# A fixed stretch of rows for every expert, row sends spread over sixteen groups, and VectorE's scans ahead of its low parts

## The reference

```python
# attention: H, DH = 16, 64; latents of 64; rotary positions on all 64 channels of a head
h = layernorm(layernorm(x)) * ln_scale + ln_bias
c_q, c_kv = h @ w_down_q.T, h @ w_down_kv.T
q, k, v = heads(c_q @ w_up_q.T), heads(c_kv @ w_up_k.T), heads(c_kv @ w_up_v.T)
attn = softmax(rope(q) @ rope(k).T / 8)
x = x + layernorm(merge(attn @ v) @ w_out.T + residual)
# experts: E, F = 8, 256, each token takes 2 of 8
z = layernorm(x)
probs = softmax(z @ router)
weights, chosen = top_k(probs, 2); weights = softmax(weights)
y = sum_e full_weights[e] * ((silu(z @ gate[e]) * (z @ up[e])) @ down[e])
x = x + layernorm(y)
```

## Time and profile before

| | us |
|---|---|
| median of 3 runs (1506.58 to 1506.79) | 1506.65 |
| the profiled execution's own time | 1505.08 |
| its span in the trace | 1502.7 |
| PE busy (93%) | 1399.5 |
| POOL busy (81%) | 1216.6 |
| DVE busy (78%) | 1166.6 |
| ACT busy (71%) | 1066.0 |

### The profile page before, as it was taken

One profiled execution on the slowest core, in us unless ns is written; L12 is line 12 of the kernel. 1 busy time (PEld: TensorE's weight loads), 2 busy tenths in 40 slices (PEclk: granted clock), 3 DMA queues, 4 the chain that ended last, 5 costly groups with the idle time before them and its releaser, 6 DMA issues. The chain is left out here.

```text
span 1502.7 us, 45158 instructions
## 1 busy us (share of the span) xinstructions
PE 1399.5 (93%) x17865; PEld 930.2 (62%) x17865; DVE 1166.6 (78%) x2685; ACT 1066.0 (71%) x2072; POOL 1216.6 (81%) x731
## 2 busy tenths in 40 slices
PE   4899999999999999999999999999999988969995
PEld 1366665666666656666665656666666555659995
DVE  7788787777788788877788788777887888945576
ACT  2677787778877877778787777777887765724444
POOL 5588898888888988889889888899789878826275
PEclk8799999999999999999999999999999999979997
DMA  5444443423233324333333323233232242133222
GB/s 169 117 114 114 114 110 84 115 69 82 65 87 83 76 72 107 79 79 79 84 86 87 79 73 88 76 82 83 72 93 67 63 160 67 44 117 99 69 53 81
DMA packets 101489, 132.87 MB, mean 88 GB/s; under 512 B 16673, under 2 KB 51233, under 8 KB 100897
## 3 DMA queue, kind: packets, MB, share of 16 engines
q1 hardware_dynamic: 98208, 123.70, 30.8%
q0 software_dynamic: 3072, 6.30, 1.4%
HBM read 20.49 MB, written 14.94 MB: 24 GB/s over the span
## 5 line engine op out<-in xcount | busy, mean ns | idle before, releaser
L1222 ACT ACTIVATE probs<-psum 128x512 f32<-128x512 f32 x1024 | 615.2, 604 | 190.3 <-PE psum L932 189.1
L1970 POOL TENSOR_TENSOR probs_lo<-probs 128x1024 f16<-128x1024 f32 x301 | 624.8, 2086 | 117.0 <-ACT probs L1222 116.0
L1518 DVE CUSTOM_DVE_ANT_0 scan_out<-psum,ahead 128x512 f16<-128x512 f32 x512 | 349.4, 686 | 199.0 <-PE psum L827 189.7
L951 PE MATMUL psum<-cv,probs 128*128 128x66 f16 x4096 | 476.3, 193 | 12.6 <-POOL probs_lo L1970 12.1
L953 PE MATMUL psum<-cv,probs 128*128 128x64 f16 x4096 | 475.9, 193 | 0.0
L955 PE MATMUL psum<-cv,probs_lo 128*128 128x66 f16 x4096 | 474.6, 192 | 0.0
L953 PEld LDWEIGHTS psum<-cv,probs 128*128 128x128 bf16 x4096 | 380.5, 97 | 110.7 <-issue 3.0
L951 PEld LDWEIGHTS psum<-cv,probs 128*128 128x128 bf16 x4096 | 385.4, 97 | 73.6 <-POOL probs_lo L1970 13.3
L930 PE MATMUL psum<-q_both,k_twice 128*128 128x512 f16 x1024 | 388.8, 380 | 2.8 <-ACT probs L1222 2.8
L932 PE MATMUL psum<-q_max,k_ones 65*128 65x512 f16 x1024 | 391.1, 382 | 0.0
L955 PEld LDWEIGHTS psum<-cv,probs_lo 128*128 128x128 f16 x4096 | 380.0, 98 | 0.0
(11 more groups left out here) (222 smaller groups left out, 1854.8 us busy)
## 6 DMA issues: line engine op xcount, KB each, us to landing
t_swapped<-t_sin SPq DMA_DIRECT2D x248, 128.0 KB, 2.0
k_twice<-qk_hi SPq DMA_DIRECT2D x128, 128.0 KB
q_lone<-qk_hi SPq DMA_DIRECT2D x64, 128.0 KB, 2.3
q_both<-qk_hi SPq DMA_DIRECT2D x64, 128.0 KB
q_both<-qk_lo SPq DMA_DIRECT2D x64, 128.0 KB
q_max<-qk_hi SPq DMA_DIRECT2D x64, 128.0 KB, 2.3
k_ones<-qk_lo SPq DMA_DIRECT2D x64, 128.0 KB, 2.4
z_unit<-slots_in SPq DMA_DIRECT2D x31, 128.0 KB, 2.3
```

What stands on the lines that cost most here:

```text
L951: pe.matmul(acc, high[:, q * P:(q + 1) * P, 1], v[:, 0:VLO], start=opens, stop=False, skip_group_check=True)
L1222: act.activation(probs[s % 4][:, i, :], score_ps[tile % SCORE_BANKS], ACT.Exp, scale=SCALE).then_inc(probs_done, 1)
L1518: dve.tensor_tensor_reduce(scan_out[m % 2][:], bank[BANK_OF["base", n, m]], ahead[m % 2][:], 1.0, LOWEST, ALU.add, ALU.max, max_all[a][:, ...
L1970: pool.tensor_tensor(probs_lo[s % 4][:].rearrange("p a n -> p (a n)"), p, p.bitcast(BF16).rearrange("p (n two) -> p n two", two=2)[:, :, 1 ...
```

## The change

The rows sent and the results now live in one HBM tensor `slots` of 26368 rows: each expert owns 3072 (`MOST_UNITS * UNIT`, as many as three batches could give it), and 1792 stand behind for the units that are not used. An expert's first row is known beforehand, so PE adds it to the ranks with one more product (`base_rows`), and `take_ranks` writes `slot_of` by itself. `place` keeps only what tells where each unit lies (`row_of`) and whose it is (`column_of`). It moves from g29 step 1 to g31 step 10 (`PLACE_AT` (7, 10)), and the ranks from group 4 step 15 of an epoch to group 5 step 10.

The sends go out two a group in g14 to g29, in steps 5 and 15 (one, in step 15, in g19 and g27), and nine each in g30 and g31. Every one but the first of a step 0 also waits for the exponentials of the steps before. From g14 to g29 DVE makes the low part of step 14 as well, a seventh; in g30 it makes eight instead of fourteen, in g31 twelve instead of sixteen, and POOL the others. In DVE's `attend`, `take_maxima` and `scan` now stand ahead of `lagged`, in every group.

SP loads and stores a unit at a row that it reads from `row_of` (one register load for four units, once for loads, once for stores). Clearing takes 26 DMAs of up to 512 KB instead of 8, four a group. The gathers wait two by two for the dense units 2, 3, ... 25.

```diff
@@ sizes, steps and places @@
+SLOTS = E * MOST_UNITS * UNIT
+ALL_SLOTS = SLOTS + (SORTED - CHOICES * MOST_UNITS) * UNIT
...
-LATE_DVE_STEPS = {GROUPS - 3: (2, 4, 6, 8, 10, 13, 15), GROUPS - 2: (0, 1, 2, 3, 5, 6, 7, 8, 9, 11, 12, 13, 14, 15),
-                  GROUPS - 1: tuple(range(STEPS))}
+SENDING = tuple(range(14, 30))
+LATE_DVE_STEPS = {**{g: DVE_STEPS + (14,) for g in SENDING}, GROUPS - 2: (1, 3, 5, 7, 9, 11, 13, 15), GROUPS - 1: (0, 1, 2, 4, 5, 6, 8, 9, 10, 12, 13, 14)}
...
-RANK_AT, PLACE_AT = (4, 15), (5, 1)
+RANK_AT, PLACE_AT = (5, 10), (7, 10)
...
-SEND_AT = ([(LAST - 2, s) for s in (11, 12, 13, 14, 15, 15)]
-           + [(LAST - 1, s) for s in range(STEPS) for _ in range(2 if s % 3 == 0 and s else 1)]
-           + [(LAST, s) for s in range(14) for _ in range(1 + s % 2)])
+SEND_AT = [(g, s) for g in SENDING for s in ((15,) if g in (19, 27) else (5, 15))]
+SEND_AT += [(g, s) for g in (30, 31) for s in (0, *range(1, STEPS, 2))]
+FIRST_GATHER = 2
@@ SP @@
             def load_unit(unit):
+                first = first_row(unit, rows_from)
...
             def store_unit(unit):
+                first = first_row(unit, rows_to)
...
-                    for piece in to_clear[2 * (r - 1):2 * r]:
-                        clear_slots(*piece)
+                    clear_slots(r, 0)
...
+                clear_slots(g, 1)
                 put_both(g + 1, 1)
@@ PE, rank_tokens @@
+                pe.matmul(dst[:, 0:own], ones[:], base_rows[:], start=True, stop=False, skip_group_check=True)
@@ DVE, take_ranks and place @@
-                dve.tensor_reduce(ranks[:, n], rank_parts[:], AX, ALU.add).then_inc(ranked, 1)
+                    dve.tensor_reduce(slot_of[:, n], rank_parts[:], AX, ALU.add).then_inc(ranked, 1)
...
+                dve.tensor_scalar(unused[:], units_of[0:1, :], -float(UNIT), float(MOST_UNITS * UNIT), ALU.mult, ALU.add)
...
+                dve.tensor_tensor(jumps[:], past[:], unused[:].unsqueeze(1).to_broadcast([1, COLUMNS, E]), ALU.mult)
...
+                step(dve.tensor_tensor(row_of[:], jump[:], steps_of[0:1, :], ALU.add), 7)
@@ DVE, attend @@
                 for s in range(STEPS):
-                    lagged(g, s, g > 0)
                     if g and s == TURN_STEPS[1]:
                         take_maxima(g, 1)
...
                         scan(g + 1, s)
+                    lagged(g, s, g > 0)
@@ POOL, sends and gathers @@
                     if (t, k) == (0, 0):
-                        pool.wait_ge(placed, 1)
+                        pool.wait_ge(ranked, n + 1)
                         pool.wait_ge(z_lo_done, CHUNKS * (n + 1))
+                    if 2 * s + i:
+                        pool.wait_ge(probs_done, g * KEY_TILES + 2 * s + i)
...
+                beside = FIRST_GATHER + made // 2
+                if made % 2 == 0:
+                    pool.wait_ge(fuse_done, SORTED + beside + 1)
+                else:
+                    pool.wait_ge(added, beside - DOWN_LAG + 1)
                 fetch(j, t, k)
```

More of the change, by code:

```diff
@@ L492, in final_place @@
             return final_bank(j)[:, at * P:(at + 1) * P]
-        to_clear = [(at, min(clear_rows, SORTED * UNIT - at)) for at in range(0, SORTED * UNIT, clear_rows)]
+        to_clear = [(at, min(clear_rows, ALL_SLOTS - at)) for at in range(0, ALL_SLOTS, clear_rows)]
         cleared, clear_set = sem("cleared"), sem("clear_set")
@@ L566, in in_dram, with unit_rows @@
             return t[bass.ds(b, 1)].rearrange("b (t p) d -> p (b t) d", p=P)
-        def unit_rows(rows, unit):
-            return rows[unit * UNIT:(unit + 1) * UNIT, :].rearrange("(i p) d -> p i d", p=P)
+        def unit_rows(first):
+            return slots[bass.ds(first, UNIT), :].rearrange("(i p) d -> p i d", p=P)
         def dense(unit):
@@ L883, in rank_tokens @@
                 own = TILES * E
+                pe.matmul(dst[:, 0:own], ones[:], base_rows[:], start=True, stop=False, skip_group_check=True)
                 for k in range(CHOICES):
-                    pe.matmul(dst[:, 0:own], above[:], hots[:, n, k].rearrange("p t e -> p (t e)"), start=k == 0, stop=False,
+                    pe.matmul(dst[:, 0:own], above[:], hots[:, n, k].rearrange("p t e -> p (t e)"), start=False, stop=False,
                               skip_group_check=True)
@@ L1668, in take_ranks, with step @@
             def take_ranks(n):
+                def step(ins, k):
+                    ins.then_inc(rank_steps, 1)
+                    dve.wait_ge(rank_steps, n + k)
                 dve.wait_ge(rank_ready, n + 1)
@@ L1674, in take_ranks @@
                     last = dve.tensor_tensor(rank_parts[:, k], before, hots[:, n, k], ALU.mult)
-                dve.tensor_copy(counts[:], src[:, TILES * E:TILES * E + E]).then_inc(rank_steps, 1)
-                dve.wait_ge(rank_steps, n + 1)
+                step(dve.tensor_copy(counts[:], src[:, TILES * E:TILES * E + E]), 1)
                 standing()
-                dve.tensor_reduce(ranks[:, n], rank_parts[:], AX, ALU.add).then_inc(ranked, 1)
+                with nc.allow_low_precision(reason="one of eight parts is not zero, and it is a whole number"):
+                    dve.tensor_reduce(slot_of[:, n], rank_parts[:], AX, ALU.add).then_inc(ranked, 1)
             place_steps = sem("place_steps")
             def place():
-                rows = EARLY * CHOICES * TILES
                 def step(ins, k):
@@ L1707, in place @@
-                step(dve.tensor_tensor(to, base_sum[:, 0:rows], ranks[:, 0:EARLY].rearrange("p b k t -> p (b k t)"),
-                                       ALU.add), 9)
+                step(dve.tensor_tensor(past[:], unit_at[:].unsqueeze(2).to_broadcast([1, COLUMNS, E]),
+                                       unit_ends[0:1, :].unsqueeze(1).to_broadcast([1, COLUMNS, E]), ALU.is_ge), 4)
+                dve.tensor_tensor(jumps[:], past[:], unused[:].unsqueeze(1).to_broadcast([1, COLUMNS, E]), ALU.mult)
@@ L1709, in place @@
+                step(dve.tensor_reduce(expert_of[:], past[:], AX, ALU.add), 5)
+                step(dve.tensor_reduce(jump[:], jumps[:], AX, ALU.add), 6)
+                dve.tensor_scalar(column_of[:], expert_of[:], float(E - 1), float(F), ALU.min, ALU.mult)
+                step(dve.tensor_tensor(row_of[:], jump[:], steps_of[0:1, :], ALU.add), 7)
                 standing()
```

66 lines of the change are left out of this document (34 added, 32 removed).

## The result

The changed kernel is slower: median 1586.12 us (4 runs, 1579.55 to 1590.2) against 1506.62 for the kernel before, a ratio of 1.053 (95% interval 1.051 to 1.055). The forecast was 1469.0, with a range of 1457 to 1485. The profiled execution took 1585.43 us with a span of 1582.3.

A forecast was written before the change was run, and what follows sets the result against it. PE was taken as the bound, apart from stalls in g29 and g30 and the hole before the sorted units; -12.2 - 7.7 - 9.5 - 11 + 3 + 0.5 - 1.5 + 0.8 = -37.6 us gave 1469.0 us, range 1457 to 1485.

The forecast's parts named there:

- The hole: Between g31 and the sorted units: PE starts 5.5 us after the group's end, not 17.66; -12.2 us.
- The clock: Start of the sorted units: shorter PE idling loses less time to the 1.2 GHz level; -1.5 us.
- g29 and g30: Both groups lose their stalls, falling to 38.0 and 36.3 us; -7.7 and -9.5 us.
- Scans ahead of low parts: g0 to g28: PE waits less for scans, turned maxima and rank sums; 60% of 18.2 us, -11 us.
- end of +5: Slow end of the scans' term in g0 to g28: +5 us if low parts come late instead.
- rival 1: Reordering only moves PE's wait to DVE's low parts or divisions; the 11 us are gone, 1480 us; chance 20%.
- keep their 1.21 to 1.26: DVE's low parts beside POOL's sends stay this short (us), so sends pay; the port rule alone would add 3 to 6 us.
- Sends and the seventh low part: g14 to g28: two sends a group, one POOL low part given to DVE, mostly covered by idle time; +3 us.
- g31: DVE makes 13 low parts instead of 16 there but also `place`, counted at 3.9 to 5 us; +0.5 us.
- The small things: SP's register loads, gathers' waits and 18 more clearing DMAs cost nearly nothing; +0.8 us for all.

The follow-up runs named there:

- e9: e8 with `place` moved in one piece to g30 step 1 and DVE making all sixteen low parts of g31; ratio 0.998 to the kernel before.
- e12: e11 with `place` cut into four parts in g30 and DVE making all sixteen low parts of g31; 1486.4 us, ratio 0.987 to the kernel before.
- e8: The changed kernel with DVE's old order (low parts ahead of scans), on a chip of usual speed; 1506.7 us, ratio 1.001 to the kernel before.
- e1: The kernel before with only DVE's reordering (scans and turned maxima ahead of low parts), on a slow chip; ratio 1.039, 61 us slower.
- e6: The kernel before with POOL's low parts only writing zeros, plus DVE's reordering; 1482.9 us, ratio 0.985 (without the reordering 1475.9 us).
- e11: e8 with one wait a group in g14 to g29: POOL's low part of step 3 waits for DVE's of step 2; 1495.2 us, ratio 0.993.
- e7: The changed kernel with POOL's low part of an odd step waiting for DVE's of the step before; 1528.1 us, ratio 1.016 to the kernel before.
- e2: The changed kernel with DVE's old order (low parts ahead of scans), on a slow chip; ratio 0.980 to the kernel before there, 27.5 us faster.

## Why the prediction was wrong, step by step

- **The hole: right in kind, and its sum partly by luck.** PE's first sorted product starts 3.5 us behind the end of g31 (1404.05); I said 5.5, and the last send within a us of the end. The send started 2.6 us ahead of it, and its landing took 3.13 us where I had 2.25. The hole shrank by 14.1 us (12.2 predicted, 13.9 at the most). SP's register load and the arithmetic take 0.8 us, from the landing of the send (1404.59) to the issue of the load (1405.35), as predicted. The chain and PE's first unit (start us, us, what):

```profile
1401.46 3.13 DMA slots<-z_rows,slot_of
...
1404.61 0.51 SPq L673
...
1407.59 0.38 PE L1046 MATMUL psum<-ident_half,z_unit 128*128 128x128 f16 x4 [0.61 <-DMA z_unit<-slots]
```

- **The clock: not as predicted.** I gave it -1.5 us in the sorted units, but they take 92.5 us (before 92.3). Their first stretch did run at a higher clock than in the earlier trace rows:

```profile
1407.59:1413.00 5.41, 4.23 (x26) 3.25 (x27) 1.61 (x4) 0.68 (x2) 0.00 (x0) 0.72 0.57 166
```

Why the whole is no shorter stays open. In e9 and e12, where the clock is 1.00 throughout, the sorted units take 91.2 us. That the part behind g31 shrank by 13.9 us in all, with 13.7 predicted, is two errors that cancel.

- **g29 and g30: right.** Without the reordering (e8) 39.2 and 35.9 us (38.0 and 36.3 predicted), with no wait of 3 us.
- **Scans ahead of low parts: the step that failed.** Predicted -11 us with an end of +5; it is +74.5 (spans of the changed kernel and e8, on two chips; e1 has +61 against its own chip's kernel before). I worked out that a low part "of 1.3 to 2.1" would be in time two steps later. These were durations of the old order, in which DVE's low part seldom began inside one of POOL's (21 of 211). Behind the scan it mostly begins when POOL's own low part is already running, and the 116 held by one take 2.2 to 2.8 us for the most part. The direction stood there as rival 1, but its price, the 11 us gone, supposed unchanged durations as well. So did the end of +5.
- **What was in the rows.** The earlier trace rows has DVE's low parts at 1207/1260/3350, one of 3.15 us. I used the long one as a cause of waits and never asked why the same instruction takes 1.22 us in one place and 3.15 in another. The sentence that low parts "keep their 1.21 to 1.26" beside sends misread that row, too: three of them that began during a send in g30 took 2.6 to 3.4 us. I did weigh the Trainium skill's rule on the shared port ("SBUF — State Buffer", section "SBUF: two separate sides"), but only for sends beside low parts. It says that a VectorE instruction with two SBUF inputs and a GpSimd one that reads SBUF exclude each other for a whole instruction, whichever begins first; my sentence had left out that the GpSimd one must read SBUF. Read for two low parts, it fits the ends of the 180, and the memsets of e6, which read nothing, agree. It goes by one instruction, and the holds of up to four in a row (6.2 us) show more. "Whichever begins first" fails beside a send, as the last section shows.
- **Sends and the seventh low part: +3 predicted, +23.4 measured (e8).** The +3 rested on POOL's idle time, 3.9 us a group. That time was not used up: POOL's waits for ACT there are 60.0 us in e8, 58.8 before (I had expected 38). 13.4 us of the 23.4 are the three holds that one wait a group takes away (e11), so what counts is where POOL pauses and not how much it idles in total. The other 10 are spread over the groups, and no wait of PE in them (e11) is longer than 1.5 us; I did not take them apart.
- **g31: +0.5 predicted, +9.4 measured (e8).** I counted `place` at 3.9 to 5 us and next to nothing for the low parts that stand behind it; with its own pieces held it took 6.3, and PE stood still for 7 us.
- **The small things: right.** g0 to g13 with 18 clears more, +1.5 us in e8; gathers every 1.25 us and 82.2 us from the first of them on.
- In sum, without the reordering I expected -26.6 us and got +5.0 of span; 29 of the 31.6 between them are the sends and g31. With it, 117 us separate forecast and result, three quarters of them (74.5 + 11) from one line moved.

## What to carry to other kernels

When an instruction's shortest and longest time differ by more than a factor of two, find what decides before moving it: here the order on one queue cost little by itself (7 us in e6), and nearly all of the rest came from when its instructions begin beside those of the other queue. If VectorE and GpSimd both read SBUF, count where each one's instructions begin beside the other's. A wait that lets the short one go first can pay (56 us in e7, 12 with one a group in e11). Work moved to a busy group is best moved in pieces (6.9 us between e9 and e12 in g30). A ratio measured on one chip may hold something of that chip: e2 had 0.980 there and 1.001 elsewhere.

## What the runs showed of the hardware that I had not expected

- DVE's low part (two SBUF inputs) is held by a running POOL instruction that reads SBUF, and ends 1.08 us behind it: all 180 over 1.3 us in the changed kernel, all 101 before. Sometimes it is held past two to four POOL instructions in a row (6.2 us at worst). What decides whether DVE gets its turn at the first end of such an instruction (174 of the 180) is open.
- The other way round, a DVE low part that begins while POOL is idle is not held: in the fourteen traces, 375 begin so and have a POOL instruction that reads SBUF begin before they end, and none of them takes over 1.3 us.
- Small instructions are held as well: `unused`, 1x8, 1.71 instead of 0.16 us; `unit_ends`, 128x8, 1.96 instead of 0.15.
- DVE instructions that read PSUM are not held. All scans and all products with the sine, in the changed kernel:

```profile
L1541 DVE CUSTOM_DVE_ANT_0 scan_out<-psum,ahead x512: 637/690/694, 38.5 to 1366.2; 128x512 f16<-128x512 f32 x171
L1529 DVE TENSOR_TENSOR t_sin<-psum,sin_sb x124: 673/680/682, 22.0 to 1307.1; 128x512 f32<-128x512 f32 x124
```

- Nor do POOL's memsets (e6), nor its sends by themselves: of the 20 low parts that begin during a send in the kernel before, 17 take 1.21 or 1.22 us. But during a send the order of the beginnings does not decide. In g30 of the kernel before:

```profile
1240.61 1.78 POOL L2005 DMA_INDIRECT slots_in<-z_rows,slot_of  x1 [0.17 <-issue]
1242.07 3.35 DVE L1539 TENSOR_TENSOR probs_lo<-probs 128x1024 f16<-128x1024 f32 x1
1242.43 1.90 POOL L1970 TENSOR_TENSOR probs_lo<-probs 128x1024 f16<-128x1024 f32 x1
```

DVE's low part begins 0.36 us ahead of POOL's, and is held through it all the same. Over all fourteen traces 15 low parts begin during a send with a POOL instruction that reads SBUF starting within 0.52 us; 14 of them are held. None is held where that instruction starts 0.66 us later or more. Why is open. `unused` in the changed kernel began 0.40 us ahead of such an instruction, during a send, too.
- On one of the chips PE stood idle among the dense units with nothing to wait for in the profile, in all four kernels run there: 9.7 to 29.2 us in all, against 0.4 in the kernel before on its usual chip. The cause is open.
